# Mixing channels with 32x32 products instead of block-diagonal 128x128 ones in a conditional mixture-of-experts layer

## What is computed

```python
att = softmax(h @ W2 + b2)                           # (64, 8)
agg_w = einsum('bk,koi->boi', att, weight[..., 0])   # one 32x32 matrix per sample
agg_b = att @ bias_k
out = einsum('boi,bih->boh', agg_w, x) + agg_b[:, :, None]
# xt = out as 2048 rows of 512
scores = softmax(xt @ router_w + router_b) + router_bias
# the best 2 of 4 groups of experts, in them the best 2 of 16 experts: idx, gate
y = sum over the chosen experts of gate * ((silu(xt @ w1 + b1) * (xt @ w2 + b2)) @ w3 + b3)
z = silu(xt @ sw1 + sb1) * (xt @ sw2 + sb2) @ sw3 + sb3
return x + y + z
```

## Time and profile before

| | us |
|---|---|
| median of 3 runs | 253.44 |
| lowest and highest | 252.91, 253.76 |
| the profiled execution, its own time | 253.9 |
| its span, first to last instruction | 252.1 |
| PE busy in the span | 241.7 (96%) |
| PE weight loads busy | 164.6 (65%) |
| DVE, ACT, POOL busy | 127.8, 78.4, 109.7 |

### The profile page before, as it was taken

One profiled execution on the slowest core, in us unless ns is written; L12 is line 12 of the kernel. 1 busy time (PEld: TensorE's weight loads), 2 busy tenths in 40 slices (PEclk: granted clock), 3 DMA queues, 4 the chain that ended last, 5 costly groups with the idle time before them and its releaser, 6 DMA issues.

```text
span 252.1 us, 4013 instructions
## 1 busy us (share of the span) xinstructions
PE 241.7 (96%) x1147; PEld 164.6 (65%) x1148; DVE 127.8 (51%) x268; ACT 78.4 (31%) x169; POOL 109.7 (44%) x128
## 2 busy tenths in 40 slices
PE   7969999999999889999999999999999999999993
PEld 7927777788875446767777777777777754444441
DVE  0193332269879887333333333333333311198995
ACT  3214555413149000333333333333333321110210
POOL 7196566410030355466666666666664331000080
PEclk9968999999999999999999999999999999999999
DMA  6999979887508938954555455455554222999974
GB/s 195 322 405 387 314 226 371 295 274 294 213 37 313 420 100 259 361 174 155 170 165 170 139 153 161 135 166 166 166 166 166 84 91 49 364 388 388 395 292 166
DMA packets 20843, 58.37 MB, mean 231 GB/s; under 512 B 2549, under 2 KB 2677, under 8 KB 20572
## 3 DMA queue, kind: packets, MB, share of 16 engines
q1 hardware_dynamic: 15228, 40.35, 44.6%
q0 software_dynamic: 5600, 17.83, 21.6%
HBM read 41.39 MB, written 17.30 MB: 233 GB/s over the span
## 4 chain that ended last, share of the span: by engine, by line
PE 87%; DVE 9%; issue 2%; DVEq 0%; ACT 0%; POOL 0%; POOLq 0%
PE psum L536 76%; PE psum L688 6%; PE psum L586 3%; DVE xT L1161 2%; PE psum L701 2%; DVE xT L910 1%; DVE xt_sb L1161 1%; DVE x_early L910 1%; DVE r L935 1%; DVE xt_sb L910 1%; DVE r L1117 0%; DVE code_f L1095 0%; DVE late_region L910 0%; ACT late_region L806 0%; DVE mix_bias L931 0%
## 5 line engine op out<-in xcount | busy, mean ns | idle before, releaser
L536 PE MATMUL psum<-wexp,r 128*128 x272 | 68.4, 381 | 0.5 <-DVE r L1117 0.4
L536 PEld LDWEIGHTS psum<-wexp,r 128*128 128x128 f32 x272 | 48.5, 190 | 22.9 <-issue 16.9
L477 POOL DMA_INDIRECT expert_rows<-late_region,to_row x33 | 33.3, 1010 | 33.5 <-ACT late_region L853 33.5
L910 DVE TENSOR_TENSOR r<-psum,ebias 128x256 f32<-128x256 f32 x34 | 14.4, 425 | 64.7 <-PE psum L536 64.7
L471 POOL DMA_INDIRECT late_region<-xt_rows,from_row x36 | 35.3, 982 | 17.1 <-issue 10.5
L536 PE MATMUL psum<-wexp,xt_sb 128*128 x68 | 34.8, 594 | 0.0
L536 PE MATMUL psum<-xT,shared_sb 128*128 128x512 f32 x64 | 28.0, 593 | 0.1
L847 ACT ACTIVATE r<-r 128x128 f32<-128x128 f32 x34 | 10.5, 309 | 55.4 <-DVE r L910 55.4
L853 ACT ACTIVATE late_region<-psum 128x512 f32<-128x512 f32 x34 | 20.3, 598 | 15.8 <-PE psum L536 15.8
L1117 DVE COPY r<-psum 128x512 f32<-128x512 f32 x36 | 24.5, 680 | 0.0
L688 PE MATMUL psum<-ident,late_region 128*128 128x128 f32 x144 | 21.6, 273 | 0.9 <-DMA late_region<-xt_rows,from_row 0.9
(11 more groups left out here) (173 smaller groups left out, 291.8 us busy)
## 6 DMA issues: line engine op xcount, KB each, us to landing
wexp<-expert_pack SPq DMA_DIRECT2D x16, 768.0 KB, 6.1
wexp<-expert_rows SPq DMA_DIRECT2D x8, 1024.0 KB, 12.8
xt_rows<-xt_sb SPq DMA_DIRECT2D x16, 256.0 KB, 3.8
x_early<-x SPq DMA_DIRECT2D x2, 1024.0 KB, 10.1
late_region<-x SPq DMA_DIRECT2D x2, 1024.0 KB, 15.0
ebias<-expert_bias SPq DMA_DIRECT2D x1, 2048.0 KB, 7.8
out_dram<-x_early SPq DMA_DIRECT2D x8, 256.0 KB, 9.6
shared_sb<-shared_pack SPq DMA_DIRECT2D x1, 1536.0 KB, 18.6
```

What stands on the lines that cost most here:

```text
L477: nc.gpsimd.indirect_dma_start(out=y_dram[:, :], out_offset=bass.IndirectOffsetOnAxis(ap=rows_of.bitcast(U32), axis=0), in_=y_sb[:, slot, ...
L536: return nc.tensor.matmul(dst, lhsT, rhs, start=start, stop=stop)
L910: return nc.vector.tensor_tensor(dst, a, b, op)
```

## The change

One 128x512 product per tile, of which three quarters of the weights are zero, becomes sixteen products of 32x32 by 32x512 per group of four tiles. Weights and data of a product lie on 32 partitions that start at 32 r, and its result goes to 32 partitions that start at 32 q of PSUM bank r. So r and q both run over 0 to 3, each product has its own 32x32 part of the array, and the four products with the same r fill bank r. A product takes sample 4 (4 g + r) + q of the batch, so bank r holds the mixed tile 4 g + r whole, in the same order as before.

For this the four samples of one tile have to lie on the same 32 partitions. So `x` is loaded in blocks: each group by four transfers to 32 partitions in place of one to 128 (256 KB each, still in pieces of 2 KB). As the early groups are also the place of the final sum, which needs the natural order, they are loaded a second time in that order (`x_natural_loaded`), behind the last store of the mixing stage. `shared_sum` waits for that.

The matrices are copied to dense places, by DVE for r = 0 to 2 and by ACT for r = 3, group by group. The four bias copies move to ACT too. The memset of `r1` falls away. A group's sixteen products write PSUM banks 0 to 3, so they wait until ACT has read all four tiles of the group before. The transposes use banks 5 and 6. Within a step PE now runs the router's products of tile s - 2 first and then the transposes of tile s.

```diff
@@ layout of the matrices
-        mixT = r1[:, :].rearrange("p (t m) -> p t m", m=P)
+        mixT = r1[:, 0:NT * IN_C].rearrange("p (g q o) -> p g q o", g=NG, q=BPT)
...
+        def copy_mixes(copy, g, r):
+            rows = slice(r * IN_C, (r + 1) * IN_C)
+            return copy(mixT[rows, g].rearrange("p q (j o) -> p q o j", o=BPT), mixes[rows, r, g])
@@ SP
-                sp.dma_start(dst, group_of_x(g)).then_inc(x_loaded[g], 16)
+                for r in range(BPT):
+                    first = (g * BPT + r) * BPT
+                    sp.dma_start(dst[r * IN_C:(r + 1) * IN_C], x[first:first + BPT].rearrange("q i d -> i q d")
+                                 ).then_inc(x_loaded[g], 16)
...
+            for g in range(EARLY):
+                sp.dma_start(x_early[:, g * GT:(g + 1) * GT, :], group_of_x(g)).then_inc(x_natural_loaded, 16)
             sp.wait_ge(b3_ready, 1)
@@ POOL
-            link(nc.gpsimd.memset(att_rows, 0.0))
-            nc.gpsimd.memset(r1[:, :], 0.0).then_inc(blocks_zeroed, 1)
+            nc.gpsimd.memset(att_rows, 0.0).then_inc(blocks_zeroed, 1)
@@ PE, the mixing stage
-                if s < NT:
-                    if s % GT == 0:
-                        pe.wait_ge(x_loaded[s // GT], 16)
-                    pe.wait_ge(mix_copied, mixes_until(s))
-                    if s >= 2:
-                        pe.wait_ge(xt_ready, s - 1)
-                    mm(psum[:, s % 2, :], mixT[:, s, :], x_tile(s)).then_inc(xt_done, 1)
-                if 1 <= s <= NT:
-                    ...
+                if s < NT and s % GT == 0:
+                    g = s // GT
+                    pe.wait_ge(x_loaded[g], 16 * BPT)
+                    pe.wait_ge(mix_copied, g + 1)
+                    pe.wait_ge(mix_copied_too, g + 1)
+                    if g > 0:
+                        pe.wait_ge(xt_ready, s)
+                    for q in range(BPT):
+                        for r in range(BPT):
+                            rows = slice(r * IN_C, (r + 1) * IN_C)
+                            last = mm(psum[q * IN_C:(q + 1) * IN_C, r, :], mixT[rows, g, q, :],
+                                      x_tile(s + q)[rows, :])
+                    last.then_inc(xt_done, GT)
                 if s >= 2:
                     ...
+                if s < NT:
+                    pe.wait_ge(xt_ready, s + 1)
...
+                    for c in range(C):
+                        last = nc.tensor.transpose(psum[:, 5 + s % 2, c * P:(c + 1) * P],
+                                                   xt_ring[:, s % RING, c * P:(c + 1) * P], ident[:, :])
+                    last.then_inc(xtT_done, 1)
@@ ACT
+            act.wait_ge(pe_cond, 5)
+            for r in range(BPT):
+                rows = slice(r * IN_C, (r + 1) * IN_C)
+                nc.scalar.activation(mix_bias[rows, :], mixes_bias[rows, r], ACT.Copy).then_inc(bias_copied, 1)
+            for g in range(NG):
+                copy_mixes(lambda dst, src: nc.scalar.activation(dst, src, ACT.Copy), g, BPT - 1
+                           ).then_inc(mix_copied_too, 1)
-                nc.scalar.activation(xt_ring[:, t % RING, :], psum[:, t % 2, :], ACT.Identity,
+                nc.scalar.activation(xt_ring[:, t % RING, :], psum[:, t % GT, :], ACT.Identity,
@@ DVE
-            for r in range(BPT):
-                rows = slice(r * IN_C, (r + 1) * IN_C)
-                V.tensor_copy(mix_bias[rows, :], mixes_bias[rows, r])
-            for first, end in MIXES:
-                for r in range(BPT):
-                    rows = slice(r * IN_C, (r + 1) * IN_C)
-                    last = V.tensor_copy(mixT[rows, first:end, rows].rearrange("p t (j g) -> p t g j", g=BPT),
-                                         mixes[rows, r, first:end])
+            for g in range(NG):
+                for r in range(BPT - 1):
+                    last = copy_mixes(V.tensor_copy, g, r)
                 last.then_inc(mix_copied, 1)
...
-                if g >= EARLY:
-                    dve.wait_ge(x_again_loaded, 16 * (NT - EARLY * GT))
+                dve.wait_ge(*((x_natural_loaded, 16 * EARLY) if g < EARLY else
+                              (x_again_loaded, 16 * (NT - EARLY * GT))))
```

More of the change, by code:

```diff
@@ L138, in adaln_moe_ffn @@
         att_max, att_sum, att_rec = early(BS, 1), early(BS, 1), early(BS, 1)
-        mixes = psum[:, 4:8, :].rearrange("p g n -> p (g n)").rearrange("p (g j t r) -> p r t g j", g=BPT, t=NT, r=BPT)
+        mixes = psum[:, 4:8, :].rearrange("p g n -> p (g n)").rearrange("p (o j g r q) -> p r g q o j", o=BPT, g=NG, r=BPT, q=BPT)
         mixes_bias = psum[:, 3, 0:BS].rearrange("p (t r) -> p r t", r=BPT)
@@ L218, in adaln_moe_ffn @@
         act_cond = sem("act_cond")
+        bias_copied = sem("bias_copied")
         mix_copied = sem("mix_copied")
+        mix_copied_too = sem("mix_copied_too")
+        x_natural_loaded = sem("x_natural_loaded")
         xt_done = sem("xt_done")
@@ L279, in adaln_moe_ffn @@
         SPLITS = EARLY * GT + 4
-        MIXES = [(0, GT), (GT, 2 * GT), (2 * GT, NT)]
         block = ctx.enter_context(nc.Block())
@@ L298, in split_of @@
             return shared_sb[:, cols], w_split[:, 0, cols], w_split[:, 1, cols]
-        def mixes_until(t):
-            return next(n + 1 for n, (first, end) in enumerate(MIXES) if first <= t < end)
+        def copy_mixes(copy, g, r):
+            rows = slice(r * IN_C, (r + 1) * IN_C)
+            return copy(mixT[rows, g].rearrange("p q (j o) -> p q o j", o=BPT), mixes[rows, r, g])
         def group_of_x(g):
@@ L570, in _ @@
             for s in range(NT + 2):
-                if s < NT:
-                    if s % GT == 0:
-                        pe.wait_ge(x_loaded[s // GT], 16)
-                    pe.wait_ge(mix_copied, mixes_until(s))
-                    if s >= 2:
-                        pe.wait_ge(xt_ready, s - 1)
-                    mm(psum[:, s % 2, :], mixT[:, s, :], x_tile(s)).then_inc(xt_done, 1)
-                if 1 <= s <= NT:
-                    t = s - 1
-                    if t == 0:
-                        pe.wait_ge(ident_ready, 1)
-                    pe.wait_ge(xt_ready, t + 1)
-                    if t >= 2:
-                        pe.wait_ge(xT_ready, t - 1)
-                    for c in range(C):
-                        last = nc.tensor.transpose(psum[:, 2 + t % 2, c * P:(c + 1) * P],
-                                                   xt_ring[:, t % RING, c * P:(c + 1) * P], ident[:, :])
-                    last.then_inc(xtT_done, 1)
+                if s < NT and s % GT == 0:
[11 more added lines that the diff above has]
+                    last.then_inc(xt_done, GT)
                 if s >= 2:
@@ L592, in _ @@
                         pe.wait_ge(router_loaded, 16)
-                        pe.wait_ge(mix_copied, len(MIXES))
                     pe.wait_ge(xT_ready, t + 1)
@@ L597, in _ @@
                                   start=(c == 0), stop=(c == C - 1))
-            last.then_inc(logits_done, 1)
+                    if t == NT - 1:
+                        last.then_inc(logits_done, 1)
+                if s < NT:
+                    pe.wait_ge(xt_ready, s + 1)
+                    if s == 0:
+                        pe.wait_ge(mix_copied, NG)
+                        pe.wait_ge(mix_copied_too, NG)
+                    if s >= 2:
+                        pe.wait_ge(xT_ready, s - 1)
+                    for c in range(C):
+                        last = nc.tensor.transpose(psum[:, 5 + s % 2, c * P:(c + 1) * P],
+                                                   xt_ring[:, s % RING, c * P:(c + 1) * P], ident[:, :])
+                    last.then_inc(xtT_done, 1)
             def shared_up(g, i, between=()):
@@ L782, in _ @@
             nc.scalar.activation(att_e, att, ACT.Exp, accum_out=att_sum).then_inc(act_cond, 1)
+            act.wait_ge(pe_cond, 5)
[5 more added lines that the diff above has]
+                           ).then_inc(mix_copied_too, 1)
+            act.wait_ge(bias_copied, BPT)
             for t in range(NT):
-                act.wait_ge(mix_copied, mixes_until(t))
                 act.wait_ge(xt_done, t + 1)
@@ L941, in _ @@
                 if t == (NG - 1) * GT:
-                    dve.wait_ge(mix_copied, len(MIXES))
+                    dve.wait_ge(mix_copied, NG)
                 V.tensor_copy(xT[:, t // GT, :, (t % GT) * P:(t % GT + 1) * P],
-                              psum[:, 2 + t % 2, :].rearrange("p (c n) -> p c n", c=C)).then_inc(xT_ready, 1)
+                              psum[:, 5 + t % 2, :].rearrange("p (c n) -> p c n", c=C)).then_inc(xT_ready, 1)
             def te(a):
```

## The result

| | before | after |
|---|---|---|
| median, us | 253.18 (252.48 to 253.76, 4 runs) | 275.91 (274.32 to 277.03, 4 runs) |
| span of the profiled execution | 252.1 | 272.6 |
| mean granted clock | 0.986 | 0.894 |

The change makes the kernel slower: 1.0888 of the time before, with a 95% interval of 1.0833 to 1.0943. The forecast was 253.0 and its range ended at 258.

A forecast was written before the change was run, and what follows sets the result against it. PE was taken to set the mixing stage's pace at 2.19 us per tile, with stores close behind. The stage would end at 52.9, 0.45 us earlier: 253.9 - 0.45 = 253.4, or 253.0 against the median; range 246 to 258.

The forecast's parts named there:

- Burst: Mixing products on PE: a group's sixteen products run side by side in 1.3 us, with ends 0.94 and 3.8.
- rival B: Mixing products: different column blocks don't run side by side, a burst takes 3.8 us, time 258.0; chance 0.22.
- Loads: Loading x to 32 partitions: 4.8 us per megabyte, 6.6 us more in all, shared weights at 30.5, store 0 at 31.1.
- Rival A: Loads of x keep the full rate, stage ends 7.0 us earlier, time 246.4; chance 0.28, with rates between.
- The clock: Mixing stage: 2 us charged for half clock after PE stands still about 10 us before tile 4's eviction.
- The 19.8: Mixing stage from tile 4's eviction at 31.1 to its end at 50.9, before the 2 us for the clock.
- rival C: Mixing stage: clock stays at half as PE waits for stores in every group; end near 68, time near 268; chance 0.08.
- C's sign: Mixing stage: the clock still at 0.50 at 45 us would show that it stays at half.
- the gain or loss of the stage goes through: Behind the mixing stage: PE's order is unchanged, so the stage's 0.45 us gain reaches the end.
- The second load of `x`: Behind the last experts' weights: 2 MB, 5.2 us at 403 GB/s, with some 20 us of cover for `ebias`.
- 253.4: Whole kernel: forecast time of the profiled execution, 253.9 - 0.45 us.

The follow-up runs named there:

- b_loads32: The kernel before with each group of x loaded by four transfers to 32 partitions, in natural order; 264.57 us.
- a_whole_half8: The changed kernel with host-blocked x in one transfer per group, an unread 256-column product per tile and eight identity products before the first burst; 250.71 us.
- a_half: The changed kernel plus five identity products before the first burst, 256 unread columns per tile, twelve products before tile 4; 259.30, 264.72, 264.92, 271.38 us.
- a_x_whole: The changed kernel with x laid out in blocks by the host and loaded by one 128-partition transfer per group; 262.96 us.
- b_warm: The kernel before with nine unread 128x128 identity products ahead of the first mixing product; 251.90 us.
- a_fill2: The changed kernel with two unread products of 256 columns added per tile; 267.08 us.
- a_fill: The changed kernel with one unread 128x512 product added per tile but the first; 264.11 us.
- b_loads32_warm: The kernel before with x by 32-partition transfers and 24 unread identity products of 128 columns in PE's stand before tile 4; 259.91 us.

## Why the prediction was wrong

**Burst: right.** Forecast 1.3 us at full clock, measured 1.14; 2.01 at half in the changed kernel. Both row and column blocks run side by side, so rival B is out. The Trainium skill's page "TensorE: Matmul & The Clock Gate", section "Part 3: Packing small matmuls", led to an estimate of 1.4. By the 15 us of sixteen products one after the other the trace shows 13 times, where that page of the Trainium skill has 10.6.

**Loads: right in kind, 2.4 us too early.** The rate was near the slow end, 217 GB/s, a megabyte in 4.8 us. But the last transfer of `x` landed at 29.4 (issued at 10.2, 19.2 us to land) and not near 25. From there to 32.9 the queue moved 391 GB/s, 1.37 MB of the 1.57 of the shared weights, so a small part of these had come beside `x`. They landed at 32.9, not 30.5, and store 0 at 33.6, not 31.1. Why `x` came later than 4.8 us per megabyte has it is open. The rule of the page "SBUF — State Buffer" of the Trainium skill, section "Door 1: The DMA port swizzle", a limit of 218 GB/s for partitions 0 to 31, agrees with the 217 of this trace; b_loads32 moved 227, somewhat more. Rival A is out.

**The clock: the step that failed.** The prediction charged "2 us, since half of what runs at half clock waits for evictions anyway". From the eviction of tile 4 to the end of the stage it gave 19.8 + 2 = 21.8 us; it took 33.3. These 11.5 us are the largest part of the miss. The 19.8 itself was sized well: in a_whole_half8, all at full clock, the same stretch took 25.4 us with twelve fillers of 0.53, which leaves 19.0. So what failed is the 2 us for the clock. Three errors lie in it. The clock was taken as back at 1.0 before the stand and as lost in it for a short time, but it fell at 14.46 and had not come back when the stand began at 28.6. I took the row before as the measure of how long a fall lasts, 6.8 us, but there 128x512 products filled 0.94 of the 2.19 us of every tile beside the router and the transposes; in the change a burst of 1.14 us per four tiles stands in their place. And at half clock nothing waits for evictions: PE is the bound with 2.45 us per tile.

The outcome is that of rival C, which had a chance of 0.08 and its stage end "near 68": it came at 66.9, and the clock was at 0.50 until 45.18, which just meets C's sign. But C's reason, "PE now waits for stores in every group", was not what happened: PE stood once, for 5.8 us. And that 68 is near 66.9 is in part luck, as C had twelve tiles at 3.1 us from 31.1 on, where it was 33.3 us from 33.6 on with 3.4 of them at full clock. What spoke against C, "the same kinds of work, only denser", was the point itself.

**What lay behind the stage: not all passed through unchanged.** "After the stage PE's order is the same, so the gain or loss of the stage goes through" was right for the order, but 2.6 us of the shared products at half clock, 2.7 at the exit of the loop and 1.6 behind it came on top. No row of before could show the exit wait; in the thirteen kernels it goes with the count of instructions. The second load of `x` was covered, as forecast: from the last of these shared products to the last product of the loop it is 127.7 us, 127.8 before.

**The sum.** 253.4 + 2.5 (loads) + 11.5 (clock in the stage) + 2.6 + 2.7 + 1.6 = 274.3, the profiled execution's 274.32. A caution: this splits the changed kernel by time, while the runs split it by cause: 13.0 us go with the 32-partition transfers, clock included, and the other 9.8 with thin work and code position.

## What to carry to other kernels

Before you take dense products out of PE, ask what will hold its clock. Read the clock row beside the busy row: here 17.00 of 17.00 us busy ran at 0.50 where PE did only 16-column products, transposes and short bursts, and unread products brought it back. A saving on PE is to be priced at the clock that the remaining work is granted, and a load at the partitions that it reaches. When "issue" appears at a loop's end after any edit upstream, shift the code by some instructions before you look for a data cause.

## What was not expected of the hardware

- The clock fell in stands of 6.8 and 6.3 us (b_loads32, a_half), but also with PE busy throughout (a_x_whole at 29.9, b_warm at 12.75). How long it stayed at half went with the work: 13.6 us in b_loads32, 30.7 in the changed kernel, and there it came back for only 3.4.
- PE waited 2.75 us at the exit of a loop, or 1.15, or 0, and the number of its instructions ahead of the loop told the cases apart. In a_x_whole, with 2.73, the clock stayed at 1.0 behind it, in the changed kernel it fell.
- A float32 pass with 64 columns takes as long as one with 128 when each loads full weights.
- Transfers to 32 partitions move 217 to 227 GB/s, with several of them in flight to different quarters at once: the fourth quarter of one group landed at 18.9 us, after the first of the next at 18.1.
- Open: why the clock fell in a_fill2 behind a stand of 1.9 us and not in a_fill behind one of 1.6. The two differ in how the same 512 columns are cut, and one profile of each can't settle it. In b_loads32_warm it fell too, 1.7 us after the end of a stand of 1.6.
